# Expert rows scaled by their gate before they are stored, and added to the token rows by the gathers

## What is computed

```python
ht = rmsnorm(x, ff_ln_w).reshape(-1, Dx)
logits = ht @ gate_w
top_vals, top_idx = jax.lax.top_k(logits, 2)
gates = jax.nn.softmax(top_vals, axis=-1)
out = jnp.zeros_like(ht)
for e in range(8):
    we = jnp.sum(gates * (top_idx == e), axis=-1)
    ye = jax.nn.silu(ht @ w1[e]) * (ht @ w3[e]) @ w2[e]
    out = out + we[:, None] * ye
x = x + out + residual          # end of layer 0
# layer 1
u = bi_wkv(x, fside, fside, w, u, cond)      # sigmoid(x) * ratio
qx = fp8(u / row_scale); g = qx @ w_gate; p = qx @ w_up; t = silu(g) * p
qt = fp8(t / row_scale); x = x + qt @ w_down
```

## Time and profile before

| | us |
|---|---|
| time, median of 3 runs | 640.15 (636.33 to 640.99) |
| the profiled execution's own time | 639.25 |
| its span, first to last instruction | 637.4 |
| busy: TensorE, VectorE, ScalarE, GpSimd | 503.2, 507.2, 361.4, 240.9 |

### The profile page before, as it was taken

One profiled execution on the slowest core, in us unless ns is written; L12 is line 12 of the kernel. 1 busy time (PEld: TensorE's weight loads), 2 busy tenths in 40 slices (PEclk: granted clock), 3 DMA queues, 4 the chain that ended last, 5 costly groups with the idle time before them and its releaser, 6 DMA issues.

```text
span 637.4 us, 10889 instructions
## 1 busy us (share of the span) xinstructions
PE 503.2 (79%) x3862; PEld 410.8 (64%) x3862; DVE 507.2 (80%) x981; ACT 361.4 (57%) x762; POOL 240.9 (38%) x204
## 2 busy tenths in 40 slices
PE   2011298789999999998579997799999999466775
PEld 1011133468888878887458997799999999333443
DVE  4999877788888888885528989478899999479992
ACT  3345245677877778875126555375565555347671
POOL 3344014844444445530645267141414350170011
PEclk9999999899999999999579999799999999788797
DMA  8300004050000000000279898679978764030001
GB/s 257 136 1 1 0 1 132 1 174 2 2 1 3 2 1 18 18 1 2 79 264 348 286 302 145 229 261 191 388 257 267 272 115 138 25 109 16 9 26 34
DMA packets 36530, 71.87 MB, mean 113 GB/s; under 512 B 5275, under 2 KB 21915, under 8 KB 36219
## 3 DMA queue, kind: packets, MB, share of 16 engines
q10 hardware_dynamic: 15280, 40.77, 20.5%
q1 hardware_dynamic: 18123, 22.26, 10.4%
q0 software_dynamic: 3072, 8.14, 4.6%
HBM read 66.03 MB, written 5.12 MB: 112 GB/s over the span
## 4 chain that ended last, share of the span: by engine, by line
PE 51%; DVE 28%; issue 7%; DMA 5%; ACT 4%; POOL 2%; SPq 1%; DVEq 0%; ACTq 0%; POOLq 0%; PEldq 0%
PE pb L437 9%; PE pw L437 8%; PE sc L478 6%; PE pb L631 5%; PE pt L631 5%; PE sc L631 4%; PE po L437 4%; PE pt L489 3%; DMA areg<-h_dram,row_ids 3%; DVE areg L1181 2%; DVE areg L1167 2%; DVE areg L1165 2%; DVE rs L1579 1%; DMA wreg<-in_L_ffn_w 1%; DVE breg L1238 1%
## 5 line engine op out<-in xcount | busy, mean ns | idle before, releaser
L1723 POOL TENSOR_TENSOR breg<-breg,con 128x512 f32<-128x512 f32 x32 | 40.8, 1274 | 80.2 <-ACT breg L864 80.2
L437 PE MATMUL pw<-areg 128*128 128x256 f16 x406 | 57.6, 276 | 3.8 <-DVE areg L1533 3.8
L437 PE MATMUL pb<-areg,wreg 128*128 128x512 f16 x240 | 58.7, 381 | 2.0 <-ACT breg L864 1.9
L872 ACT ACTIVATE breg<-breg,mx 128x128 f32<-128x128 f32 (+1 forms) x128 | 56.6, 445 | 1.6 <-DVE mx L1289 1.6
L631 PE MATMUL pb<-areg,wreg 128*128 128x128 f32 x448 | 54.0, 279 | 0.6 <-ACT areg L965 0.6
L478 PE MATMUL sc<-areg,breg 128*128 128x128 f32 (+1 forms) x256 | 48.9, 335 | 5.6 <-DVE mx L1289 4.3
L631 PEld LDWEIGHTS pb<-areg,wreg 128*128 128x128 f32 x448 | 52.6, 196 | 0.9 <-issue 0.8
L631 PE MATMUL pt<-areg,wreg 128*128 128x128 f32 x424 | 49.9, 275 | 1.5 <-DMA wreg<-in_L_ffn_w 1.5
L631 PEld LDWEIGHTS pt<-areg,wreg 128*128 128x128 f32 x424 | 48.5, 192 | 1.7 <-DMA wreg<-in_L_ffn_w 1.6
L631 PE MATMUL sc<-areg,wreg 128*128 128x128 f32 x416 | 48.9, 275 | 0.0
L631 PEld LDWEIGHTS sc<-areg,wreg 128*128 128x128 f32 x416 | 47.6, 192 | 0.1
(11 more groups left out here) (250 smaller groups left out, 1291.1 us busy)
## 6 DMA issues: line engine op xcount, KB each, us to landing
wreg<-in_L_ffn_w ACTq DMA_DIRECT2D x40, 896.0 KB, 7.2
wreg<-in_L_ffn_w SPq DMA_DIRECT2D x14, 896.0 KB, 8.4
ys_dram<-areg ACTq DMA_DIRECT2D x23, 128.0 KB, 5.9
wreg<-in_L_ffn_wq SPq DMA_DIRECT2D x1, 2048.0 KB, 9.4
wreg<-in_L_ffn_wo SPq DMA_DIRECT2D x1, 2048.0 KB, 8.2
areg<-in_fside_BxSxS ACTq DMA_DIRECT2D x4, 256.0 KB, 5.5
x_in<-in_x SPq DMA_DIRECT2D x4, 256.0 KB, 4.7
h_dram<-areg SPq DMA_DIRECT2D x8, 128.0 KB, 1.7
```

The lines of the kernel that those rows point to most:

```text
L437: last = nc.tensor.matmul(bank, w(a), m(b), start=first and k == 0, stop=final and k == 2)
L872: last = nc.scalar.activation(pr[:, parity, b, o:o + w], pr[:, parity, b, o:o + w], ACT.Exp, bias=mx[:, parity, k:k + 1], scale=-1.0, accu ...
L1723: G.tensor_tensor(t2[:, parity, :].rearrange("p (b n) -> p b n", b=2), t2[:, parity, :].rearrange("p (b n) -> p b n", b=2), rope_sin.rearr ...
```

## The change

The gate goes into the row before it is stored, and the two rows are added on the way into the token rows.

- Behind the two casts, VectorE makes the tile one-hots anew, splits each gate into a high and a low fp16 part and multiplies them into the one-hots (`hot_gate`). TensorE multiplies 16 times more (46 columns), ahead of the filler; VectorE adds the parts to one gate for each slot, over WS (`slot_gate`).
- ScalarE's copy of an expert tile takes its column of `slot_gate` as scale.
- GpSimd's gathers add into the token rows. The two gathers of one row must not overlap, so the second of a group is issued after the first has landed; the first of the next group is put between.
- `combine` and `y12` are gone; ScalarE's sigmoid and TensorE's first filler of the tail wait for the gathers themselves.

```diff
--- before.py
+++ after.py
@@ -30,6 +30,7 @@
 IQ = 88
 NI = INTER // IQ
 IH = INTER // 2
+GATE_LOW = 2048.0
 WS = 64.0
 EPS = 1e-5
 QKV = (H + 2 * KVH) * HD
@@ -144,7 +145,6 @@
         h2 = cut(areg, 14336, NT * D).rearrange("p (i n) -> p i n", i=NT)
         h2T = cut(areg, 16384, 2 * D).rearrange("p (k n) -> p k n", k=2)
 
-        y12 = cut(areg, 0, 2 * NT * D).rearrange("p (k i n) -> p k i n", k=2, i=NT)
         qx = cut(areg, 4224, 2 * D, F16).rearrange("p (k i n) -> p k i n", k=2, i=2)
         qxT = cut(areg, 8576, D, F16).rearrange("p (k c n) -> p k c n", k=2, c=C)
         qt = cut(areg, 4864, INTER // 2, F16)
@@ -185,6 +185,10 @@
         hot_place = cut(breg, 2048, NT * P, F16).rearrange("p (k n) -> p k n", n=P)
         hot_tile = cut(breg, 4096, NT * MT, F16).rearrange("p (k n) -> p k n", n=MT)
 
+        hot_gate = cut(breg, 4288, 2 * NT * MT, F16).rearrange("p (k s n) -> p k s n", s=2, n=MT)
+        gate_high = cut(breg, 4672, NT, F16).rearrange("p (k i) -> p k i", k=2)
+        gate_low = cut(breg, 4688, 2 * NT).rearrange("p (k i) -> p k i", k=2)
+
         rows = cut(breg, 0, 2048)
         grid = cut(breg, 2048, 2048)
         rq = cut(breg, 4096, 1024, F16)
@@ -230,6 +234,7 @@
         place = sb("place", [P, 2, 2 * NT], I32)
         placef = sb("placef", [P, 2, 2 * NT])
         row_ids = sb("row_ids", [P, MT], I32)
+        slot_gate = sb("slot_gate", [P, MT])
         h2_dram = nc.dram_tensor("h2_dram", (NT * P, D), F32).ap()
         scale_dram = nc.dram_tensor("scale_dram", (2 * INTER + D,), F32).ap()
         ys_dram = nc.dram_tensor("ys_dram", (SLOTS, D), F32).ap()
@@ -248,14 +253,14 @@
             "av_done ohi_done olo_done zeros_ready wo_step wo_done x1a_done "
 
             "ssq2_ready rstd2_ready h2_ready h2T_done h2T_copied gate_tile d_ready ge_ready mk_ready rank_done tmap_ready "
-            "cmp_ready hot_ready ids_done ids_ready identb_ready "
+            "gates_split slot_gates slot_gate_ready cmp_ready hot_ready ids_done ids_ready identb_ready "
 
             "rq_ready rqT_done rq_copied ratio1_copied wscale_ready xsum_ready "
 
             "w_ready xT_done xT_copied upa_done upb_done silu_a_done silu_b_done inner_a_done inner_b_done "
             "inner_high inner_low tmi_ready w2hi_done w2lo_done down_done y_copied "
 
-            "x1_ready sgx_ready qx_ready qxT_done qxT_copied gatep_done upp_done gate_ready inner_ready "
+            "sgx_ready qx_ready qxT_done qxT_copied gatep_done upp_done gate_ready inner_ready "
             "inv_ready scaled_ready fold_ready fold_high fold_low xinv_ready xout_ready xscaled_ready qt_ready qtT_done qtT_copied dn_done yo_read yo_ready").split()
         s = {n: sem(n) for n in names}
         s_f = [sem(f"f_in{b}") for b in range(B)]
@@ -576,6 +581,11 @@
                     pe.wait_ge(s["hot_ready"], k // NT + 1)
                 last = nc.tensor.matmul(pw[:, 0:MT], hot_place[:, k, :], hot_tile[:, k, :], start=k == 0, stop=k == 2 * NT - 1)
             last.then_inc(s["ids_done"], 1)
+            pe.wait_ge(s["gates_split"], 1)
+            for k in range(2 * NT):
+                last = nc.tensor.matmul(pt2[:, 0, 0:2 * MT], hot_place[:, k, :], hot_gate[:, k].rearrange("p s n -> p (s n)"),
+                                        start=k == 0, stop=k == 2 * NT - 1)
+            last.then_inc(s["slot_gates"], 1)
             keep_clock(pt2[:, 1, :], 12)
 
 
@@ -655,6 +665,8 @@
                 if n < MT:
                     pe.wait_ge(s_u[n % SLOTS_UP], 32 * (n // SLOTS_UP + 1))
                     pe.wait_ge(s["xT_copied"], n + 1)
+                    if n == 1:
+                        pe.wait_ge(s["slot_gate_ready"], 1)
                     up(n, parity, 0)
                 if n + 1 < MT:
                     x_transposes(n + 1, (n + 1) % 4, x_slot.get(n))
@@ -724,7 +736,7 @@
             pe.wait_ge(s["fold_high"], 2)
             pe.wait_ge(s["fold_low"], 2)
             pe.wait_ge(s["inner_low"], 2 * MT)
-            pe.wait_ge(s["x1_ready"], 1)
+            pe.wait_ge(s_g[0], 32)
             keep_clock(pt2[:, 1, :], 10)
             quantised_transposes(0)
             gate_products(0)
@@ -987,6 +999,7 @@
 
             for k in range(2):
                 act.sem_inc(s_y[k], 16)
+            act.wait_ge(s["slot_gate_ready"], 1)
 
             x_slot, y_slot = side_pieces(ratio_piece, weight_piece, down_piece)
             def fold_high(m):
@@ -1025,7 +1038,8 @@
                     if n in y_slot:
                         y_slot[n](pw)
                     act.wait_ge(s_y[1 - parity], 16 * ((n + 1) // 2))
-                    nc.scalar.activation(ysb[:, 1 - parity, :], pw[:, 0:D], ACT.Copy, scale=1.0 / WS).then_inc(s["y_copied"], 1)
+                    nc.scalar.activation(ysb[:, 1 - parity, :], pw[:, 0:D], ACT.Copy, scale=slot_gate[:, n - 1:n])\
+                        .then_inc(s["y_copied"], 1)
                     act.wait_ge(s["y_copied"], n)
                     act.dma_start(ys_dram[(n - 1) * P:n * P, :], ysb[:, 1 - parity, :]).then_inc(s_y[1 - parity], 16)
                 if n in (20, 21):
@@ -1034,8 +1048,8 @@
 
             def input_gate(g):
 
-                act.wait_ge(s["x1_ready"], g + 1)
                 first, count = GROUPS[g]
+                act.wait_ge(s_g[g], 32 * count)
                 nc.scalar.activation(xsig[:, first:first + count, :], x1[:, first:first + count, :], ACT.Sigmoid).then_inc(s["sgx_ready"], 1)
 
             def copy_qxT(i):
@@ -1430,6 +1444,25 @@
             dve.wait_ge(s["identb_ready"], 1)
             dve.sem_inc(s["tmap_ready"], 1)
 
+            link(V.tensor_tensor(hot_tile, iota_t.rearrange("p (a n) -> p a n", a=1).to_broadcast([P, 2 * NT, MT]),
+                                 over(placef[:, 0, :], MT), ALU.is_equal))
+            for k in range(2):
+                last = V.tensor_copy(gate_high[:, k], gts[:, :, 3 + k])
+            link(last)
+            for k in range(2):
+                last = V.tensor_tensor(gate_low[:, k], gts[:, :, 3 + k], gate_high[:, k], ALU.subtract)
+            link(last)
+            link(V.tensor_scalar(gate_low, gate_low, GATE_LOW, None, ALU.mult))
+            for k in range(2):
+                tiles = hot_tile[:, k * NT:(k + 1) * NT]
+                V.tensor_tensor(hot_gate[:, k * NT:(k + 1) * NT, 0], tiles, over(gate_high[:, k], MT), ALU.mult)
+                last = V.tensor_tensor(hot_gate[:, k * NT:(k + 1) * NT, 1], tiles, over(gate_low[:, k], MT), ALU.mult)
+            last.then_inc(s["gates_split"], 1)
+            dve.wait_ge(s["slot_gates"], 1)
+            link(V.tensor_copy(slot_gate[:, :], pt2[:, 0, 0:MT]))
+            link(V.scalar_tensor_tensor(slot_gate[:, :], pt2[:, 0, MT:2 * MT], 1.0 / GATE_LOW, slot_gate[:, :], ALU.mult, ALU.add))
+            V.tensor_scalar(slot_gate[:, :], slot_gate[:, :], 1.0 / WS, None, ALU.mult).then_inc(s["slot_gate_ready"], 1)
+
             def round_e4m3(link, dst, v, g):
 
                 link(V.tensor_scalar(g.bitcast(I32), v.bitcast(I32), 0x7F800000, None, ALU.bitwise_and))
@@ -1559,19 +1592,9 @@
 
 
             dve.wait_ge(s["xsum_ready"], 1)
+            dve.wait_ge(s["fold_low"], 2)
             dve.wait_ge(s["ratio1_copied"], B)
             dve.wait_ge(s["scale_in"], 32)
-
-            def combine(g):
-
-                first, count = GROUPS[g]
-                dve.wait_ge(s_g[g], 32 * count)
-                for k in range(2):
-                    for i in range(first, first + count):
-                        last = V.scalar_tensor_tensor(x1[:, i, :], y12[:, k, i, :], gts[:, i, 3 + k:4 + k], x1[:, i, :], ALU.mult, ALU.add)
-                    if k == 0:
-                        link(last)
-                last.then_inc(s["x1_ready"], 1)
 
             def scale_of_rows(at, value, i, n, done):
 
@@ -1631,19 +1654,14 @@
                 V.scalar_tensor_tensor(yo[:, k, :], pw[:, 0:D], rs[:, 7, i:i + 1], srow[:, 2 * INTER:], ALU.mult, ALU.mult)\
                     .then_inc(s["yo_read"], 1)
 
-            combine(0)
             mix_input(0)
-            combine(1)
             round_input(0)
             mix_input(1)
             round_input(1)
-            combine(2)
             inner_rows(0)
             inner_rows(1)
             round_inner(0)
             mix_input(2)
-            combine(3)
-            combine(4)
             round_input(2)
             round_inner(1)
             mix_input(3)
@@ -1826,20 +1844,27 @@
             pool.wait_ge(s["u_used"], 2 * B)
             pool.wait_ge(s_y[0], 16 * ((MT + 1) // 2 + 1))
             pool.wait_ge(s_y[1], 16 * (MT // 2 + 1))
-            def gather_group(g):
+            pool.wait_ge(s["xsum_ready"], 1)
+
+            def add_expert_rows(g, k):
                 first, count = GROUPS[g]
+                if k == 1:
+                    pool.wait_ge(s_g[g], 16 * count)
                 for i in range(first, first + count):
-                    for k in range(2):
```

(12 more changed lines are left out.)

## The result

The changed kernel takes 648.76 us (median of 4 runs, 647.07 to 651.06) where the kernel before took 639.2 beside it: ratio 1.0139, 95% interval 1.0109 to 1.0168. It is slower, by 9 us and not by the 3.9 of the forecast. The profiled execution is 648.38 long (before: 639.25, so 9.1 less), its span 646.5 at a mean granted clock of 0.939 (before: 637.4 at 0.947). Executions of one kernel agree within some 1%; a single one, of experiment e2, was far slower (681.9) and is left out of every number.

A forecast was written before the change was run, and what follows sets the result against it. The prediction took TensorE to bound the expert tiles and VectorE the tail. It added 3.2 (front), 0.2 (copies' scale) and 0.5 (tail), +3.9 on 639.25, for 643.2 us; range 637.5 to 652 for 8 in 10 runs.

The forecast's parts named there:

- Part 1: Ahead of the expert tiles: gate work delays TensorE's first transposes by 3.8 us, of which 3.2 reaches the whole.
- The cover at the second tile's weights: Expert tiles' start: TensorE's 1.45 us wait for the second tile's weights takes its shift of 3.8 down to 2.35.
- the front is swallowed: Rival, expert tiles: TensorE's 8.6 us wait for a gathered token tile shrinks by the delay, giving 640.0; chance 0.13.
- Part 2: ScalarE's expert-tile copies: a column as scale adds 0.1 us twice on the path, +0.2 (0 to 0.3).
- Part 3: Gathers at the tail's start: second waits for first, each landing 3.2 after issue, so mixing begins 2.0 us later.
- a: Tail's start: the delay of the start of mixing, put at +2.0 us (1.0 to 2.8).
- Just in time: Tail: the sixth gather, completing tile 1, lands at 565.8, when ScalarE's sigmoid (about 565.9) and VectorE's mixing (566.4) want it.
- before anyone asks: Tail: the last gather starts near 575.3 and lands at 578.5, before its rows are wanted.
- The rival of the costly gather: Rival, tail: adding gathers cost GpSimd more; a period over 1.6 us decides, 2.2 gives 650.7; chance 0.20.
- 4 us of room: Tail, against the costly gather: at an unchanged period the last gather lands at 578.5, wanted at 582.5.
- Part 4: Tail: of 7.1 us of removed combining only 1.5 is gained; with the later start of mixing, +0.5 (-0.5 to +1.3).
- the tail pays as VectorE's share suggests: Rival, tail: combining behind tile 0 is all gain, 6.2 us, giving 637.5, or 634 with front covered; chance 0.12.

The follow-up runs named there:

- e2: The kernel before with only the new tail (adding gathers, their orders and waits) and no gate on the rows: 645.3 us, ratio 1.009.
- f6: The changed kernel with only the gathers' order altered, row tile 1's second gather issued fourth instead of sixth: 652.2 us, ratio 1.0176.
- e3: The changed kernel with ScalarE's wait for the slot gates moved to just ahead of its first scaled copy: 648.17 us, ratio 1.0142.
- e1: The changed kernel's front alone (gates in the expert rows), with the earlier tail of plain gathers and combining with factor one: 643.78 us, ratio 1.0084.
- x15: Gates in the expert rows, filler shared out around the gate wait, ScalarE's wait late; earlier tail with all combining at factor 1: ratio 1.0014 against the kernel before.
- f7: The changed kernel with the old constant scale in ScalarE's expert-tile copies, slot gates computed but unused: 648.93 us, ratio 1.0145.
- g10: The changed kernel with 21 more filler products on TensorE at the start of the tail: 648.51 us, ratio 1.0149.
- e4: The changed kernel with gathers that copy instead of add, same order and waits: 642.01 us, ratio 1.0056.
- g12: The changed kernel with covered front, plain gathers and combining for tiles 0 to 3, adding for 4 to 7, ScalarE's copy before its last sigmoid: 637.8 us, ratio 0.9961.
- f8: The changed kernel with adding gathers of 64 rows instead of 128; a single execution, no whole time or ratio given.
- g11: g10 with ScalarE's copy of row tile 2's transposes put ahead of its last sigmoid: 647.86 us, ratio 1.0103.
- x14: The same kernel as g12, timed once more beside x15: 638.26 us, ratio 0.998 against the kernel before.

## Why the prediction was right and wrong

**Right: the direction, and what carries it.** A delay ahead of the expert tiles is paid, the long wait for the ninth token tile does not swallow it, and a tail in which VectorE is the busiest engine does not give back the 7.1 us of combining. 648.76 lies in the range of 637.5 to 652.0. **Wrong: the size**, +0.5% where +1.4% was measured, and the chance: over 646.6 had 0.27. Between the two profiled executions the sum had +3.9 and the measurement has +9.1. The tail is 5.1 longer where Parts 3 and 4 had 0.5, the expert part 5.0 longer where Parts 1 and 2 had 3.4, and 1.1 was gained ahead of the change. So the tail is 4.6 of the miss of 5.2.

**Part 1** had the place, and was short in size. TensorE got the gates at 324.96, some 2.9 us behind VectorE's cast of the identity (forecast 2.5), and the 16 products took 0.79 for 0.8. The filler took 4.08 in the profiled execution and not 5.2, so the transposes moved by 2.8; in f6, where it took 5.17, they moved by 3.85, the +3.8 of the text. The cover at the second tile's weights was there. Missed was the silu table: before, it loads in ScalarE's wait for the first products, and with a wait for the gates queued ahead it loads behind them, 1.28 on VectorE's path, which e3 took off the path again with nothing to be measured in the whole. At the wait for the ninth token tile the nine profiles with the uncovered front stand 83.7 us behind the row ids on average (82.0 to 85.7), the eight without it or with it covered 79.7 (79.1 to 80.2): +4.0, where I had +3.2 (0 to 3.8). Timed, the front costs 0.84% or 5.4 us (e1; 4.0 to 6.7) where Parts 1 and 2 had 3.4, and 0.14% or 0.9 us is left of that when it is covered (x15). Two things were not in the sum, the table load and the wait for ScalarE's copy told under f7; neither could be timed by itself. The rival "the front is swallowed" is out. The prediction had also said that it would be wrong altogether if the expert part changed its length by more than 1 us. Behind the ninth token tile it did, from 151.4 to 153.9; but e2, with the old front, has 153.3, so this sign can't tell a wrong mechanism from what lies between executions.

**Part 2**, +0.2 for the scale, is too small for the runs: f7 shows no effect, within 0.5%.

**Part 3 is the step that failed**, in two terms and in two sentences that hang on them. The term "GpSimd's time unchanged, 0.96" is 1.57 (period 1.85, not 1.27), and the landing taken at 3.2 is 3.8, above the upper of the two single-pass bounds, 3.6. By themselves the first two gathers made a = 2.7 (9.14 - 6.45), near the upper end given: the two landings took 3.90 and 3.70, and GpSimd's restart in between 0.3 where 0.7 was taken, which hid 0.4 of it. Then the sixth gather: it starts 10.4 behind the landing of the expert rows and not 8.4, and completes tile 1 at 14.3, not 11.6. "Just in time" became a wait of 2.0 for VectorE, mixing of tile 1 is 4.5 late where 2.0 was expected, and TensorE, idle meanwhile, lost another 1.4 to 2 at 1.2 GHz (after against g10: I0 21.46 and 20.07, I1 24.61 and 22.57). And "before anyone asks": the last gather was to start 13 issues of 1.27 after the second, at 575.3; it starts at 587.33, 29.2 behind the landing and not 21.1, and lands near 591.1, just as ScalarE gets to its last two sigmoids (from 591.04).

The rival of the costly gather had this mechanism and its threshold: a period over 1.6 decides. It is 1.85. The rival's own numbers were for 2.2, and a linear step down from them (13 x 1.85 + 3.8 + 4.7 = 32.6 behind the landing, where the last tiles were wanted at 28.4) gives 4.2 of the tail's 5.1. With the front's 3.4 that would have been 646.9. I gave it 0.20. Against it stood "4 us of room", which was worked out with the very period that the rival disputes, and a DMA share of 0.12, which says nothing of GpSimd's own time. The Trainium skill's ratio of 1.93 for a transfer that reduces (*Collectives: The Full Stack*, "The bandwidth ceiling") is one of bandwidths of large transfers. It is not met by these small ones: the landing grew by a factor of 1.36 and GpSimd's work by 1.64.

**Part 4** stands. The value behind the start of mixing was put at 1.5 instead of 3.5 for the eight combinings in a row; e4 has 1.55 from M0 to M3. Part of such a gain can come from elsewhere: in g12, where tiles 0 to 3 keep their combining, M0 to M3 is 1.85 shorter than before, 0.8 of it by the constant factor and 1.1 by the gathers of tiles 4 to 7. The rival "the tail pays as VectorE's share suggests" is out: even plain gathers without any combining (e4) gave 2.2 us of tail, not 5.2. The term was right and could not help, as M0 to M3 is 28.0 after, 2.2 longer than before.

**Open.** Where the filler took over 5 us (f6, f8, g11; 4.1 to 4.5 in the other six), the ninth tile came 2.9 later than in those, though the first transposes were only 0.9 later. And the expert part behind the ninth tile differs by up to 3 us between executions, of one kernel too (g12 154.3, x14 151.6). The thirteen executions with the wait for ScalarE's copy have 153.9 on average and the four without it 152.2; why the wait is there in some is not shown.

## What to carry to other kernels

Price a DMA that adds as an operation of its own: both its time on the engine that issues it and its landing. Multiply the first by the number of transfers before you call any of them "in time". Let it take work off an engine only where the consumer comes late enough; the first tiles of a stage, where everyone waits, keep the plain form. Where taking away one bound gives nothing, look for the second that ends at the same time, and try both removed. Filler that keeps the clock belongs into a new wait and not behind it. When a variant replaces an operand by a constant, measure that by itself before you credit the rest of the edit.

## What the runs showed of the hardware

- A gather of 128 rows of 1 KB that adds in SBUF: 1.57 us of GpSimd, 3.8 to landing, 144 packets; the plain one 0.96, 2.8 and 48. The adding one with 64 rows: 1.45, 3.2 and 80 (f8).
- GpSimd restarted 0.3 us after the landing of its own gather (558.85 + 3.90 to 563.01), where it took 0.7 after the landing of ScalarE's store. Taken at 0.7 in the forecast.
- With one more semaphore wait ahead of it, ScalarE's silu and its table load of 1.28 us both stood behind TensorE's first products (the load at 334.41). Without that wait the load stood ahead of them (328.75 before, 331.61 in e3).
- VectorE's `scalar_tensor_tensor` of 128x256 fp32 takes 480 ns with a column of SBUF as factor and 420 with a constant (before, x15). ScalarE's copy of 128x256 out of PSUM takes 0.47 us with a column as scale and 0.38 with a constant (after, f7).
- TensorE's granted clock was 0.84 of full speed from 570 to 575 us and 0.50 from 575 to 580. Ahead of that it had been idle for 1.94 us, had run eight products, and been idle for another 1.82. The next eight products took 2.55 us instead of 1.36.
